# Working the gate of the values in pieces of two token tiles instead of whole-batch instructions, in a one-core attention and mixture-of-experts kernel

## The reference, cut to what matters

```python
x = x + attn(layernorm(x))        # B, S, E = 8, 1024, 256
x = x + experts(layernorm(x))

def attn(x):
    Q, K, V = ...                              # 16 heads of 16
    attn = softmax(causal(Q @ K.T) * scale)
    h = x @ dp_w1 + dp_b1                      # 256 -> 128
    h = (h - mean(h)) / sqrt(var(h) + 1e-5) * ln_g + ln_b
    drift = gelu(h) @ dp_w2 + dp_b2            # 128 -> 1
    g = gelu(drift * g_w1 + g_b1)              # 1 -> 16
    gate = tanh(g @ g_w2 + g_b2)               # one number per key token
    out = (attn * gate over the keys) @ V
    return out @ Wo + bo
```

## The kernel before, in words

| item | engine | what | lines |
|---|---|---|---|
| GA | VectorE | 8 statistics, 8 aggregations, + epsilon | L1466, L1470, L1473 |
| GB | GpSimd | minus the mean, the power -1/2, their product | L1068, L1069, L1072 |
| GC | ScalarE | 8 normalisations of 128 columns | L1250 |
| GD | GpSimd | times ln_g, plus ln_b, 1024 columns each | L1079, L1082 |
| GE | ScalarE | one gelu over 1024 columns | L1269 |
| GF | GpSimd | times dp_w2, 1024 columns | L1088 |
| GG | VectorE | sum over 128 features, + dp_b2 | L1477, L1479 |
| GH | GpSimd | times g_w1, plus g_b1, 128 columns each | L1093, L1097 |
| GI, GJ, GK, GL | ScalarE, GpSimd, VectorE, ScalarE | gelu, times g_w2, sum, tanh | L1273, L1103, L1483, L1279 |

## Time and profile before

### The profile page before, as it was taken

One profiled execution on the slowest core, in us unless ns is written; L12 is line 12 of the kernel. 1 busy time (PEld: TensorE's weight loads), 2 busy tenths in 40 slices (PEclk: granted clock), 3 DMA queues, 4 the chain that ended last, 5 costly groups with the idle time before them and its releaser, 6 DMA issues.

```text
span 1826.8 us, 34347 instructions
## 1 busy us (share of the span) xinstructions
PE 1667.4 (91%) x12734; PEld 997.3 (55%) x12734; DVE 1297.7 (71%) x2528; ACT 1084.0 (59%) x1808; POOL 767.8 (42%) x1126
## 2 busy tenths in 40 slices
PE   7798899989987999899998899999998989998798
PEld 4343356435643566456554555555664656666677
DVE  4867777967796678777686666778678657873556
ACT  2565755665556656575557756576556756568432
POOL 4424432452236211632227862353116773057760
PEclk9698999989998999999998999989999899999899
DMA  4566545554345544544434765544435674346430
GB/s 152 160 192 182 164 153 157 164 149 125 99 122 137 142 121 119 158 118 141 140 113 143 213 180 143 146 125 122 132 102 152 199 204 142 94 138 203 141 121 13
DMA packets 192707, 261.24 MB, mean 143 GB/s; under 512 B 19616, under 2 KB 127264, under 8 KB 192544
## 3 DMA queue, kind: packets, MB, share of 16 engines
q1 hardware_dynamic: 181792, 229.67, 42.9%
q0 software_dynamic: 10752, 29.37, 5.5%
HBM read 130.98 MB, written 127.40 MB: 141 GB/s over the span
## 4 chain that ended last, share of the span: by engine, by line
PE 44%; DMA 16%; DVE 13%; POOL 8%; ACT 7%; SPq 5%; issue 5%; DVEq 0%; POOLq 0%; ACTq 0%
PE ps_all L2017 9%; PE ps_all L1907 7%; DVE mx L1496 6%; DMA qk_s<-ql 5%; PE ps_all L2048 5%; PE ps_all L1855 5%; ACT probs L1307 4%; PE ps_all L1887 4%; PE ps_all L1839 3%; DMA xa<-in_x 3%; PE ps_all L1916 2%; PE ps_all L1825 2%; SPq L889 2%; DMA yab<-ys_s,slot_u 2%; POOL xs_s L1157 2%
## 5 line engine op out<-in xcount | busy, mean ns | idle before, releaser
L1496 DVE TENSOR_REDUCE mx<-ps_all 128x2 f32<-128x1024 f32 (+2 forms) x640 | 616.9, 1005 | 131.1 <-PE ps_all L1862 71.2
L1307 ACT ACTIVATE probs<-ps_all 128x1024 f32<-128x1024 f32 x576 | 569.2, 1027 | 185.6 <-PE ps_all L1887 182.4
L1125 POOL TENSOR_SCALAR_AFFINE_SELECT probs<-probs 128x512 f32<-128x512 f32 x256 | 160.2, 641 | 569.4 <-ACT probs L1307 567.9
L1907 PE MATMUL ps_all<-probs,vaug 128*32 128x512 f32 (+3 forms) x3072 | 323.6, 521 | 25.2 <-POOL probs L1125 22.0
L1855 PE MATMUL ps_all<-k_st,q_st 63*128 63x512 f32 (+3 forms) x1536 | 306.3, 432 | 32.5 <-DVE mx L1496 12.1
L1887 PE MATMUL ps_all<-q_st,k_st 64*128 64x512 f32 (+3 forms) x1536 | 264.2, 404 | 45.0 <-DVE mx L1496 18.5
L1855 PEld LDWEIGHTS ps_all<-k_st,q_st 63*128 63x128 f32 x1536 | 155.1, 198 | 155.4 <-issue 52.4
L1887 PEld LDWEIGHTS ps_all<-q_st,k_st 64*128 64x128 f32 x1536 | 131.3, 193 | 173.9 <-issue 67.5
L1751 DVE SCALAR_TENSOR_TENSOR act_t<-act_t,ps_all 128x256 f32<-128x256 f32 x168 | 70.4, 419 | 151.8 <-ACT act_t L1370 150.9
L2017 PE MATMUL ps_all<-w_hi,x2h 128*128 128x512 f32 (+1 forms) x480 | 167.7, 349 | 2.5 <-DVE ql L1458 1.2
L2017 PE MATMUL ps_all<-w_hi,x2l 128*128 128x512 f32 (+1 forms) x480 | 157.8, 329 | 0.0
(11 more groups left out here) (195 smaller groups left out, 2810.1 us busy)
## 6 DMA issues: line engine op xcount, KB each, us to landing
qk_s<-qh SPq DMA_DIRECT2D x116, 256.0 KB
q_st<-qk_s SPq DMA_DIRECT2D x128, 192.0 KB, 3.9
k_st<-qk_s SPq DMA_DIRECT2D x128, 192.0 KB, 4.7
xs<-xs_s SPq DMA_DIRECT2D x72, 256.0 KB
ys_s<-ysb SPq DMA_DIRECT2D x72, 256.0 KB, 3.5
o_s<-o_sb SPq DMA_DIRECT2D x64, 256.0 KB, 4.4
qk_s<-ql SPq DMA_DIRECT2D x57, 256.0 KB
xs_s<-ysb SPq DMA_DIRECT2D x20, 512.0 KB, 5.5
```

The source lines that it names most:

```text
L1125: last = nc.gpsimd.affine_select(out=block, in_=block, compare_op=ALU.is_ge, fill=0.0, base=0, pattern=[[0, GROUP], [1, P]], channel_multi ...
L1307: nc.scalar.activation(to, of, ACT.Exp, scale=DH ** -0.5).then_inc(freed[release[item][0]], 1)
L1496: last = nc.vector.tensor_reduce(to[:, :, p, qt % QPC], both[:, :, at:at + keys], X_AXIS, ALU.max)
L1907: last = mm(bank(first)[32 * h:32 * h + 32, q0 - c * CHUNK:], vaug[:, kt, g, h * VW:h * VW + 32], probs[:, s % 2, h, at:at + cols], start= ...
```

## The change

Four gate items become four pieces each, of two token tiles (`PIECES` = 4): the statistics GA, the normalisations GC, the multiply-add pair GD and the product GF. Aggregation and epsilon leave GA and become an item of their own, GS. The gelu GE stays one instruction over the whole batch, as do GG and all that follows. A GA piece depends only on its own two AB items; a GD piece only on its own GC piece; GE waits for the last GD piece. The planner's costs are new too: GB 2270 instead of 2000, GD 4 x 1300 instead of 4800, GF 4 x 680 instead of 2400, GA 4 x 450 + 700 instead of 2510, GC 4 x 780 instead of 3090. Semaphore counts follow.

```diff
+PIECES = TILES // QT
...
-        add("DVE", ("GA", n), 2510, due, [("AB", n, t) for t in range(TILES)])
-        add("POOL", ("GB", n), 2000, due, [("GA", n)])
-        add("ACT", ("GC", n), 3090, due, [("GB", n)])
-        add("POOL", ("GD", n), 4800, due, [("WC",), ("GC", n)])
-        add("ACT", ("GE", n), 3600, due, [("GD", n)])
-        add("POOL", ("GF", n), 2400, due, [("GE", n)])
-        add("DVE", ("GG", n), 1430, due, [("GF", n)])
+        for i in range(PIECES):
+            add("DVE", ("GA", n, i), 450, due, [("AB", n, t) for t in range(i * QT, (i + 1) * QT)])
+        add("DVE", ("GS", n), 700, due, [("GA", n, PIECES - 1)])
+        add("POOL", ("GB", n), 2270, due, [("GS", n)])
+        for i in range(PIECES):
+            add("ACT", ("GC", n, i), 780, due, [("GB", n)])
+            add("POOL", ("GD", n, i), 1300, due, [("WC",), ("GC", n, i)])
+        add("ACT", ("GE", n), 3600, due, [("GD", n, PIECES - 1)])
+        for i in range(PIECES):
+            add("POOL", ("GF", n, i), 680, due, [("GE", n)])
+        add("DVE", ("GG", n), 1430, due, [("GF", n, PIECES - 1)])
...
-            def gate_scale(item, n):
+            def gate_scale(item, n, i):
...
-                if first_wait("g_act", n * 4 + 1):
-                    pool.wait_ge(g_act, n * 4 + 1)
-                nc.gpsimd.tensor_tensor(hidden, hidden, ln_g[:].unsqueeze(1).to_broadcast([P, TILES, DP]),
+                if first_wait("g_act", n * G_ACT + i + 1):
+                    pool.wait_ge(g_act, n * G_ACT + i + 1)
+                piece = hidden[:, i * QT:(i + 1) * QT, :]
+                nc.gpsimd.tensor_tensor(piece, piece, ln_g[:].unsqueeze(1).to_broadcast([P, QT, DP]),
                                         ALU.mult).then_inc(g_pool, 1)
...
-                nc.gpsimd.tensor_tensor(hidden, hidden, dp_w2[:].unsqueeze(1).to_broadcast([P, TILES, DP]),
+                piece = hidden[:, i * QT:(i + 1) * QT, :]
+                nc.gpsimd.tensor_tensor(piece, piece, dp_w2[:].unsqueeze(1).to_broadcast([P, QT, DP]),
                                         ALU.mult).then_inc(g_pool, 1)
...
-            def gate_norm(item, n):
-                act.wait_ge(g_pool, n * 8 + 2)
-                for t in range(TILES):
+            def gate_norm(item, n, i):
+                if first_wait("g_pool", n * G_POOL + 2):
+                    act.wait_ge(g_pool, n * G_POOL + 2)
+                for t in range(i * QT, (i + 1) * QT):
...
-            def gate_stats(item, n):
-                b, k = release["AB", n, TILES - 1]
+            def gate_stats(item, n, i):
+                b, k = release["AB", n, (i + 1) * QT - 1]
                 dve.wait_ge(freed[b], k)
-                for i in range(TILES):
-                    last = nc.vector.bn_stats(st_g[:, i, :], hidden[:, i, :])
+                for t in range(i * QT, (i + 1) * QT):
+                    last = nc.vector.bn_stats(st_g[:, t, :], hidden[:, t, :])
                 last.then_inc(g_dve, 1)
-                dve.wait_ge(g_dve, n * 6 + 1)
+
+            def gate_means(item, n):
+                dve.wait_ge(g_dve, n * G_DVE + PIECES)
```

More of the change, by code:

```diff
@@ L740, in build @@
         N_CONST = 10
+        G_POOL, G_DVE, G_ACT = 5 + 3 * PIECES, PIECES + 5, PIECES + 3
         def bank(item, j=0):
@@ L1062, in rstd_a @@
                 nc.gpsimd.tensor_tensor(mv_a[:, ts, 0], mv_a[:, ts, 0], rs_a[:, ts], ALU.mult).then_inc(a_rstd, 1)
-            G_POOL = 8
             def gate_rstd(item, n):
-                pool.wait_ge(g_dve, n * 6 + 3)
+                pool.wait_ge(g_dve, n * G_DVE + PIECES + 2)
                 nc.gpsimd.tensor_tensor(mv_g[:, :, 0], mv_g[:, :, 0], minus_one[:], ALU.mult).then_inc(g_mean, 1)
@@ L1072, in gate_rstd, with gate_dot1 @@
                 nc.gpsimd.tensor_tensor(mv_g[:, :, 0], mv_g[:, :, 0], rs_g[:], ALU.mult).then_inc(g_pool, 1)
-            def gate_scale(item, n):
-                if n == 0:
+            def gate_scale(item, n, i):
+                if n == 0 and i == 0:
                     pool.wait_ge(wc_in, 7 * 16)
-                if first_wait("g_act", n * 4 + 1):
-                    pool.wait_ge(g_act, n * 4 + 1)
-                nc.gpsimd.tensor_tensor(hidden, hidden, ln_g[:].unsqueeze(1).to_broadcast([P, TILES, DP]),
+                if first_wait("g_act", n * G_ACT + i + 1):
+                    pool.wait_ge(g_act, n * G_ACT + i + 1)
+                piece = hidden[:, i * QT:(i + 1) * QT, :]
+                nc.gpsimd.tensor_tensor(piece, piece, ln_g[:].unsqueeze(1).to_broadcast([P, QT, DP]),
                                         ALU.mult).then_inc(g_pool, 1)
-                pool.wait_ge(g_pool, n * G_POOL + 3)
-                nc.gpsimd.tensor_tensor(hidden, hidden, ln_b[:].unsqueeze(1).to_broadcast([P, TILES, DP]),
+                pool.wait_ge(g_pool, n * G_POOL + 2 + 2 * i + 1)
+                nc.gpsimd.tensor_tensor(piece, piece, ln_b[:].unsqueeze(1).to_broadcast([P, QT, DP]),
                                         ALU.add).then_inc(g_pool, 1)
-            def gate_dot1(item, n):
-                if first_wait("g_act", n * 4 + 2):
-                    pool.wait_ge(g_act, n * 4 + 2)
-                nc.gpsimd.tensor_tensor(hidden, hidden, dp_w2[:].unsqueeze(1).to_broadcast([P, TILES, DP]),
+            def gate_dot1(item, n, i):
+                if first_wait("g_act", n * G_ACT + PIECES + 1):
+                    pool.wait_ge(g_act, n * G_ACT + PIECES + 1)
+                piece = hidden[:, i * QT:(i + 1) * QT, :]
+                nc.gpsimd.tensor_tensor(piece, piece, dp_w2[:].unsqueeze(1).to_broadcast([P, QT, DP]),
                                         ALU.mult).then_inc(g_pool, 1)
             def gate_hidden(item, n):
-                pool.wait_ge(g_dve, n * 6 + 5)
+                pool.wait_ge(g_dve, n * G_DVE + PIECES + 4)
                 nc.gpsimd.tensor_tensor(gt[:], drift[:].unsqueeze(2).to_broadcast([P, TILES, GH]),
@@ L1095, in gate_hidden @@
                                         ).then_inc(g_pool, 1)
-                pool.wait_ge(g_pool, n * G_POOL + 6)
+                pool.wait_ge(g_pool, n * G_POOL + 3 + 3 * PIECES)
                 nc.gpsimd.tensor_tensor(gt[:], gt[:], g_b1.unsqueeze(1).to_broadcast([P, TILES, GH]),
@@ L1100, in gate_dot2 @@
             def gate_dot2(item, n):
-                if first_wait("g_act", n * 4 + 3):
-                    pool.wait_ge(g_act, n * 4 + 3)
+                if first_wait("g_act", n * G_ACT + PIECES + 2):
+                    pool.wait_ge(g_act, n * G_ACT + PIECES + 2)
                 nc.gpsimd.tensor_tensor(gt[:], gt[:], g_w2.unsqueeze(1).to_broadcast([P, TILES, GH]),
@@ L1108, in build_values @@
                     pool.wait_ge(ones_set, K_HALVES + 1)
-                if first_wait("g_act", n * 4 + 4):
-                    pool.wait_ge(g_act, n * 4 + 4)
+                if first_wait("g_act", (n + 1) * G_ACT):
+                    pool.wait_ge(g_act, (n + 1) * G_ACT)
                 if n:
@@ L1267, in gelu1 @@
             def gelu1(item, n):
-                act.wait_ge(g_pool, n * 8 + 4)
+                act.wait_ge(g_pool, n * G_POOL + 2 + 2 * PIECES)
                 nc.scalar.activation(hidden, hidden, ACT.Gelu).then_inc(g_act, 1)
             def gelu2(item, n):
-                act.wait_ge(g_pool, n * 8 + 7)
+                act.wait_ge(g_pool, n * G_POOL + 4 + 3 * PIECES)
                 nc.scalar.activation(gt[:], gt[:], ACT.Gelu).then_inc(g_act, 1)
             def gate_tanh(item, n):
-                act.wait_ge(g_dve, n * 6 + 6)
+                act.wait_ge(g_dve, (n + 1) * G_DVE)
                 if first_wait("va_built", n * GROUPS):
@@ L1471, in gate_stats @@
                 last.then_inc(g_dve, 1)
-                dve.wait_ge(g_dve, n * 6 + 2)
+                dve.wait_ge(g_dve, n * G_DVE + PIECES + 1)
                 nc.vector.tensor_scalar(ve_g[:], mv_g[:, :, 1], EPS, None, ALU.add).then_inc(g_dve, 1)
             def gate_drift(item, n):
-                dve.wait_ge(g_pool, n * 8 + 5)
+                dve.wait_ge(g_pool, n * G_POOL + 2 + 3 * PIECES)
                 nc.vector.tensor_reduce(drift[:], hidden, X_AXIS, ALU.add).then_inc(g_dve, 1)
-                dve.wait_ge(g_dve, n * 6 + 4)
+                dve.wait_ge(g_dve, n * G_DVE + PIECES + 3)
                 nc.vector.tensor_scalar(drift[:], drift[:], dp_b2, None, ALU.add).then_inc(g_dve, 1)
             def gate_sum(item, n):
-                dve.wait_ge(g_pool, n * 8 + 8)
+                dve.wait_ge(g_pool, (n + 1) * G_POOL)
                 nc.vector.tensor_reduce(drift[:], gt[:], X_AXIS, ALU.add).then_inc(g_dve, 1)
@@ L1787, in _ @@
             all_work(dve, "DVE", {"AS": stats_a, "AG": means_a, "AE": epsilon_a, "AB": values,
-                                  "QL": queries_keys, "GA": gate_stats, "GG": gate_drift, "GK": gate_sum,
+                                  "QL": queries_keys, "GA": gate_stats, "GS": gate_means, "GG": gate_drift, "GK": gate_sum,
```

## The result

| | before | after |
|---|---|---|
| median, 12 runs each on one chip | 1828.87 us | 1809.26 us |
| ratio, 95% interval | | 0.9902 [0.9882, 0.9921] |
| again, on another chip (e7 below) | 1852.15 us | 1831.07 us, 0.9905 [0.9880, 0.9929] |

The change makes the kernel 1.0% faster, on both chips. The ratios are those on record with their intervals; the quotients of the medians, 0.9893 and 0.9886, lie inside them. The time is inside the stated range, 1806 to 1847 us, 3 us from its lower end, and outside the half per cent that I took as likeliest.

The account below looks back on a forecast made before the run. The kernel was taken as bound by TensorE and what keeps it from being fed. Terms -2.4 - 2.4 + 1.2 - 0.7 + 2.3 = -2.0 us gave a span of 1824.8, plus 1.8 a median of 1826.6 us; range 1806 to 1847.

Parts of the forecast that it names:

- The pieces' prices: GpSimd's gate products: 0.74 us per 256-column piece, 14.0 us more busy time; 1.3 us left behind VectorE's last bias add.
- VectorE's held epsilons: VectorE's small epsilon held by a running GpSimd product, 1.73 instead of 0.17 us; shorter gate pieces counted as 0.
- The long stalls: GpSimd's four stalls, 4.48 to 5.62 us, at every 14th indirect DMA, expected again at the same counts.
- a rival with 0.11: The 15th and 29th indirect DMA come ahead of no mask PE wants: 9.3 us more gained, 1817.3 us, chance 0.11.
- the two waits that I named: PE's waits of 3.73 and 5.53 us for masks behind GpSimd's stalls at the 15th and 29th indirect DMA.
- VectorE's wait ahead of GG: VectorE's 6.9 us idle until GF is done, forecast 2.4 us longer; half put on PE's path, +1.2 us.
- ScalarE's ahead of GE: ScalarE's wait until GD is done, forecast shorter, as GC and GD in step end 1.2 us sooner: -2.4 us.
- the parts of my sum that need no new order: Gate terms: -2.4 for GC and GD in step, +1.2 for GF's delay, +2.3 for GD's added GpSimd time.
- the rival that isn't felt: Planner sets pieces side by side, so VectorE's -2.4 and the last batch's -0.7 fall away: 1829.7 us, chance 0.11.
- What isn't in the sum: the order: The planner places everything behind the first gate anew; left unpriced, with four GpSimd stalls as the nearest measure.
- VectorE's bound: Limit for GA in pieces, 8 x 1.2 = -9.6 us if each GA stood on the path; forecast itself -2.4.
- the covered stalls: Part of the range's lower end: -9.3 us if GpSimd's first two long stalls stand ahead of no wanted mask.

Follow-up runs that it names:

- e7: The changed kernel measured again on another chip, the one used for e5: 1831.07 us against 1852.15 for before, ratio 0.9905 [0.9880, 0.9929].
- e6: The kernel of before, unchanged, run once for its trace on the chip of e5: one execution, 1846.03 us.
- e1: Pieces of GA, GC, GD and GF set side by side in the old order of before: 1849.43 against 1842.94 us, ratio 1.0033 [1.0007, 1.0060].
- e10: The kernel of before with GA alone in pieces (GS its own item), all else whole, newly planned: ratio 0.9930 [0.9903, 0.9957] to before.
- e2: The new order of after, with each whole instruction standing where its last piece stood: ratio 0.9958 [0.9934, 0.9982] to before.
- e9: The changed kernel with GA planned whole and GC, GD, GF in pieces, newly planned: ratio 1.0028 [1.0004, 1.0052] to before.
- e3: The kernel of before with no pieces, its planner told only the costs of after, so another order: ratio 1.0037 [1.0015, 1.0059] to before.
- e11: The changed kernel, planner told GD 1500 instead of 1300 and GF 760 instead of 680 per piece: ratio 1.0041 [1.0017, 1.0064] to before.
- e5: The kernel of before with 53 empty matmuls set ahead of four sums where PE waited for a mask: ratio 0.9956 [0.9935, 0.9976] to before.
- e12: The changed kernel with 46 empty matmuls ahead of six PE items that wait: ratio 0.9911 [0.9880, 0.9943] to before.
- e4: The kernel of before with 2304 instead of 2048 bytes for GpSimd's DMA descriptors, items' order untouched: ratio 0.9948 [0.9924, 0.9972] to before.

## Why the prediction was right or wrong

**The pieces' prices were right.** GD and GF pieces take 0.737, 0.730 and 0.731 us against my 0.74, GpSimd's busy time is 780.5 against 782, table loads stay 33, and behind the last bias add there are 1.36 us against 1.3. By the Trainium skill, "GPSIMD Engine Reference", section 3.1, whose row is for an addition of 2048 elements, a piece of 256 elements would have taken near 0.68 us, an estimate by that page's rate with a fixed part of 0.12 from the trace's 2.367 us at 1024 columns; the traced 0.737 is 0.06 more. The longest of VectorE's held epsilons fell from 1.73 to 0.34 us, once in the run. VectorE's busy time moved by 3.7 us and ScalarE's by 3.2, a little more than the 3 that I allowed.

**The long stalls were right in count**, 15th, 29th, 43rd and 57th, and that a new order could cover them was a rival with 0.11. It came in for the two waits that I named, which went from 9.3 to 2.2 us. Over the run the waits for masks fell by 3.3 us only, and in e6 and e7 they rose by 2.4, so it isn't shown that this is where the gain lies.

**The effects around the gate were wrong, both ways.** VectorE's wait ahead of GG went from 6.9 to 14.6 us, not by 2.4; ScalarE's ahead of GE went from 8.7 to 10.7 us over the eight batches, and from 9.2 to 8.3 in e6 and e7, so that no shortening is shown. e1 measures the parts of my sum that need no new order: I had +1.1 for them (-2.4 + 1.2 + 2.3, the rival that isn't felt), and it is about +6 us, 5 more. If GD's and GF's added time is the cause, some 6 to 8 of its 14.0 us are on the path and not the 3.5 that I gave it; e1's added low-clock time would explain as much, and no run tells the two apart.

**The step that failed is "What isn't in the sum: the order".** I named it, put it at zero and bounded it by four stalls. By five new plans of nearly the same items, and by one of them with whole instructions, the time lay at -0.98% (after), -0.70% (e10), -0.42% (e2, after's order), +0.28% (e9), +0.37% (e3) and +0.41% (e11): a spread of 1.4% or 25 us, where the largest term that I summed was 2.4. e10, with the pieces that I had priced at -2.4 us and bounded at -9.6, gave -12.9. I had written that the order decided if PE's busy time moved by more than 10 us; it moved by 18.2, and by 12.9 without the empty matmuls. That the time fell into my range all the same is in part luck: the lower end was made of VectorE's bound, with each GA on the path, and of the covered stalls, and not of the clock or of another order.

**A missing term is the clock.** I priced a stall of PE at its own length. In both pairs of traces more of the gain stands in the time of the useful matmuls (12.9 and 8.6 us) than in idle time and empty matmuls (7.2 and 6.9), and half of the low-clock time that went (19 and 12 us) is enough to cover it. e5 shows that the fall behind a wait goes when the wait is filled, and that the time falls with it. But the clock isn't the whole: e3, e9 and e11 ran slower than before with 8, 8 and 4 us less of low-clock time, as means over their executions.

**What stays open.** Which of the many moved items make this order good isn't settled; e10 says that VectorE's pieces open the way to a good one, but e9 to e11 are one order each, and another draw could turn them. The number of the kernel's own empty matmuls differs with the plan too (70 in after, 84 in before, 89 in e10, 78 in e9, 105 in e3, 104 in e11), and no run holds it fixed. Nor is it settled how much of a given low-clock stretch is on the path. In its trace e11 has 155 us of it, and e12, on the same chip with after's order, 150; their spans are 17.1 us apart, of which 10.2 are idle time and empty matmuls and 6.9 the useful ones.

## What to carry to other kernels

Where a planner orders the work, a cut of one item into pieces is a new order of all of them: price the pieces, but expect the time to follow the order, and run the same plan with its numbers changed a little before crediting the idea. Separate the two by putting pieces into the old order and whole items into the new one. Look for a stall that returns at a fixed count, and see that nothing urgent stands behind it. And before reading busy time as work, take out what the kernel only does to keep an engine busy: here its amount follows the plan.

## What the runs showed of the hardware

With 2048 bytes of descriptor space GpSimd stalled ahead of the 15th, 29th, 43rd and 57th indirect DMA, for up to 6.3 us (e10), and with 2304 bytes ahead of the 16th, 31st and 61st, for up to 3.2 us in e4. Later ones keep the distance but not the count from the start: 2.12 us each in before at the 111th and the 175th, 14 behind the first ones of their batches, which became the 112th and the 176th in e4, and at the 125th. The stall was shorter where the DMAs ahead of it were spread out (1.15 us in after, 4.48 before, at the 15th). And in the trace of before the clock stood at its lower level from some 390 to 396 us, behind the wait of 3.73 us that ended at 388.57. In e6 the same stretch of 15 us has a mean of 0.66, and with empty matmuls in the wait's place, in e5, 1.00.
